# The opening of the causal attention layer: key-side bias tiles made by TensorE transposes of the query-side ones, one 2 MB trip through DRAM on SyncE's queue, rows of x ahead of the bias

## The chip, the cores and the metric

One core of a Trainium2 chip runs the whole program. The metric is the device time of one execution in microseconds (us); the median of three executions before the change is 2824.74 us.

## What is computed

Eight layers in a row on x of 4 x 1024 x 128: a scan layer, an expert layer, a landmark attention layer, an expert layer, **a causal attention layer with rotary positions and a relative bias**, an expert layer, a memory attention layer, an expert layer. The change lies in the fifth alone:

```python
q, k, v = heads(x @ Wq + bq), heads(x @ Wk + bk), heads(x @ Wv + bv)   # x normalised first; 16 heads of 8
q, k = q * cos + rotate_half(q) * sin, k * cos + rotate_half(k) * sin
bias = rel_bias_table[bucket(pos_i - pos_j)]                           # 32 buckets, 16 heads
att = (q @ k.T + bias) / sqrt(8), causal mask, softmax
x = x + (att @ v) @ Wp + bp
```

## The kernel before

The layers follow one another, each between barriers of all engines, so what one layer saves at its start the program saves. X stays in SBUF as `g.X`, with mean and variance of its rows in `g.MV`.

The causal layer (`causal_layer`, from L1040) works in 16 units `u`: 4 sequences times 4 groups of 4 heads. TensorE (PE), VectorE (DVE), ScalarE (ACT) and SyncE (SP, which issues the DMAs) each run the same `walk` of steps in the same order, each with its own body for a step. Two PSUM slots of two banks, `slot(n)`, are used in turn by all steps that carry a number n; PE claims a slot when the step two before has freed it.

- `turn_x`: DVE makes the normalised rows `xn` of one sequence (L1510; POOL does it for the later three, L1291), PE turns them (L1393), ACT copies them into `xt` (L1316).
- `project`: PE multiplies by Wq or Wk and its swapped copy (L1400), DVE adds bias and rotation (L1520) and sums (L1525) into `full`.
- `split`: ACT and DVE cut `full` into three bf16 pieces (L1326, L1532, L1329, L1536), and SP stores each piece in DRAM (L1239).
- `stack`: SP waits until the six pieces of the sequence are stored, then loads the operands of one unit as 72 rows for the query side (three DMAs, L1252) and 72 for the key side (three, L1255) into `stacks`.
- `values`: PE makes v (L1407), ACT copies it (L1333).
- `top`: 32 steps a unit; PE makes scores of 128 queries (L1419), DVE takes their maxima, far part by L1566 and near part with the bias `bias_q` by L1567. `join` and `lower` bring the maxima into the stacks as three further rows (L1585, L1425, L1262).
- `scores`, `products`, `copy_y` and so on: scores with bias, exp, times v.

The opening is the walk up to `lower(0)`: x of sequence 0, q and k, the stacks of units 0 to 2, v, and the 32 tops of unit 0, which nothing overlaps. Units 1 to 15 have their tops between the scores of the unit before.

The bias needs tiles whose row p is the bias vector of a head shifted by p. PE picks the vectors from the table by a one-hot product for two sides (L1380), DVE copies them (L1497, L1498), SP stores them in DRAM (L1267). ACT then copies DRAM to DRAM with one row of 1 KB for each shift, in four DMAs of 1 MB: half of the heads at a time, side 1 and side 0 (L1305). SP loads them in two halves (`load_bias`, L1232): `bias_q` for the maxima and two key-side parts, the even heads for `bias_k` (kept in `pt`) and the odd heads for `bias_kd`. Half 0 is loaded ahead of the walk; half 1 after the stack loads of unit 0. ACT and DVE cut `bias_k` into three bf16 pieces `bias_kp` for PE to add (L1310, L1541, L1312, L1544), half 0 in `values`, half 1 on DVE in the middle of the tops of unit 0 (`t == ROWS // 2`).

## Time and profile before

| | |
|---|---|
| median of 3 executions | 2824.74 us (2817.64 to 2830.39) |
| the profiled execution | 2821.07 us, its span 2819.1 us |
| busy share of the span | PE 80%, DVE 65%, PE weight load 58%, ACT 51%, POOL 31% |
| mean granted clock of TensorE | 0.865 of full speed |
| causal layer, first instruction to last statistics | 819.2 to about 1686 us |
| its opening, up to PE's step of `lower(0)` | 819.2 to 921.7 us |
| the other stretch, up to 1690 us | 768.3 us |

Times of the trace are microseconds from the start of the span. A gap of an engine stands in brackets with what ended it. DMA share is the busy share of the core's 16 DMA engines.

### The profile page before, as it was taken

What the parts mean: (1) busy time and instruction counts of PE and PEld (TensorE: products, weight loads), DVE (VectorE), ACT (ScalarE), POOL (GpSimd) and SP (SyncE); (2) the same over time, 40 slices, a digit from 0 to 9 for tenths busy, and PEclk for the clock granted to TensorE, in tenths of its full rate; (3) what the DMA queues carried; (4) which work ended last, traced back from release to release, by engine and by line L of the source; (5) the groups of instructions that cost most, each with busy time, mean ns of one, the idle gap of its engine ahead of it and who ended that gap; (6) DMA issues with size and microseconds to landing.
All of it is one profiled execution on the core that took longest, in us unless ns stands there. A gap on an engine that the chain in (4) does not pass through costs nothing. (4 is left out here: it accounts for less than half of the span.)

```text
span 2819.1 us, 79607 instructions
## 1 busy us (share of the span) xinstructions
PE 2250.5 (80%) x30676; PEld 1640.9 (58%) x30676; DVE 1820.5 (65%) x5861; ACT 1425.0 (51%) x3583; POOL 865.8 (31%) x852
## 2 busy tenths in 40 slices
PE   6489947589934888798888877948888888888786
PEld 3389924479921333333333337936777777777686
DVE  5533356633335777777777633359999999999533
ACT  4366632366621445445454544635555555555264
POOL 2157620057741100000000002624444444443255
PEclk8589977689965898989989886969999999999688
DMA  3011120011135211111110001121111111111113
GB/s 123 30 38 49 47 68 0 30 35 49 48 126 153 74 32 35 29 30 35 33 43 18 18 3 47 46 84 50 51 50 49 48 50 45 48 48 47 41 39 90
DMA packets 81721, 139.72 MB, mean 50 GB/s; under 512 B 18691, under 2 KB 37803, under 8 KB 78924
## 3 DMA queue, kind: packets, MB, share of 16 engines
q1 hardware_dynamic: 62244, 101.88, 11.6%
q0 software_dynamic: 13824, 28.34, 3.5%
q8 instruction: 250, 4.10, 0.6%
q10 hardware_dynamic: 5288, 4.46, 0.5%
q14 instruction: 115, 0.94, 0.1%
HBM read 69.69 MB, written 35.18 MB: 37 GB/s over the span
## 5 line engine op out<-in xcount | busy, mean ns | idle before, releaser
L1353 ACT ACTIVATE ca_pt<-ca_ps 128x512 f32<-128x512 f32 (+3 forms) x768 | 341.1, 491 | 369.6 <-PE ca_ps L1445 168.2
L668 PE MATMUL ffn_ps<-ffn_xst,ffn_up_w 128*128 128x128 f32 x3456 | 430.0, 279 | 0.2 <-issue 0.2
L668 PEld LDWEIGHTS ffn_ps<-ffn_xst,ffn_up_w 128*128 128x128 f32 x3456 | 411.8, 196 | 1.2 <-issue 1.2
L782 DVE TENSOR_TENSOR ffn_hid<-ffn_sg,ffn_ps 128x512 f32<-128x512 f32 x216 | 148.5, 688 | 363.1 <-PE ffn_ps L668 360.2
L540 POOL DMA_INDIRECT ffn_xs<-ffn_x,ffn_token_at x216 | 209.1, 968 | 256.7 <-DVE ffn_token_at L765 192.1
L1419 PE MATMUL ca_ps<-ca_stacks 72*128 72x512 bf16 (+3 forms) x768 | 230.1, 367 | 64.9 <-DVE ca_m_near L1567 31.3
L1774 POOL TENSOR_TENSOR im_pt_e<-im_pt,im_own 128x512 f32<-128x512 f32 x128 | 162.6, 1270 | 384.9 <-DVE im_pt L2027 367.0
L1441 PE MATMUL ca_ps<-ca_stacks 75*128 75x512 bf16 (+3 forms) x768 | 254.0, 354 | 19.2 <-ACT ca_pt L1353 11.2
L1566 DVE TENSOR_REDUCE ca_m_far<-ca_ps 128x1 f32<-128x128 f32 (+5 forms) x384 | 236.6, 616 | 47.1 <-PE ca_ps L1419 45.5
L545 POOL DMA_INDIRECT ffn_y<-ffn_ys,ffn_result_at x216 | 212.6, 984 | 153.7 <-DVE ffn_ys L788 146.1
L1567 DVE CUSTOM_DVE_ANT_0 ca_spill<-ca_ps,ca_bias_q 128x256 f32<-128x256 f32 (+1 forms) x512 | 200.7, 397 | 35.8 <-PE ca_ps L1419 35.8
L1463 PE MATMUL ca_ps<-ca_pt,ca_vp 128*9 128x512 f32 (+3 forms) x1536 | 181.9, 548 | 43.2 <-ACT ca_ysb L1361 43.2
L509 POOL MEMSET ffn_later<- 128x128 f32 x4 | 0.8, 206 | 697.0 <-POOLq L42 697.0
L1781 POOL TENSOR_TENSOR im_rope_qk<-im_t,im_mates 128x512 f32<-128x512 f32 x128 | 170.6, 1333 | 56.8 <-DMA im_mates<-im_t 56.0
L1419 PEld LDWEIGHTS ca_ps<-ca_stacks 72*128 72x128 bf16 x768 | 67.9, 103 | 199.6 <-DVE ca_m_near L1567 100.2
L1580 DVE TENSOR_TENSOR ca_ps<-ca_ps,ca_bias_kd 128x256 f32<-128x256 f32 (+1 forms) x288 | 109.8, 382 | 98.1 <-PE ca_ps L1441 94.6
L1807 ACT ACTIVATE im_ot<-im_ps 128x256 f32<-128x256 f32 x128 | 49.1, 383 | 241.4 <-PE im_ps L1870 241.4
L598 ACT ACTIVATE ffn_up_w<-w_w 128x1024 f32 x144 | 151.9, 1056 | 29.3 <-issue 26.8
L1441 PEld LDWEIGHTS ca_ps<-ca_stacks 75*128 75x128 bf16 x768 | 78.9, 103 | 146.2 <-ACT ca_pt L1353 71.9
L591 ACT ACTIVATE ffn_sg<-ffn_ps 128x512 f32<-128x512 f32 x216 | 128.9, 597 | 59.9 <-PE ffn_ps L668 59.8
L1821 ACT ACTIVATE im_pe_<-im_s,im_nm 128x32 f32<-128x32 f32 x512 | 157.0, 316 | 1.9 <-DVE im_nm L2036 1.9
L676 PE MATMUL ffn_ps<-w_w,ffn_hid 128*128 x1152 | 152.4, 276 | 1.2 <-DVE ffn_ys L788 1.2
(318 smaller groups left out, 4873.0 us busy)
## 6 DMA issues: line engine op xcount, KB each, us to landing
im_mates<-im_t SPq DMA_DIRECT2D x256, 128.0 KB
ca_stacks<-scratch_piece SPq DMA_DIRECT2D x96, 192.0 KB
ffn_got<-ffn_y SPq DMA_DIRECT2D x48, 256.0 KB, 5.7
ffn_x<-ffn_xn SPq DMA_DIRECT2D x32, 256.0 KB, 2.0
scratch_piece<-ca_piece SPq DMA_DIRECT2D x24, 256.0 KB, 2.9
w_w<-in_L_ffn_experts_w_dram SPq DMA_DIRECT2D x2, 2048.0 KB, 12.4
scratch_toeplitz<-scratch_bias ACTq DMA_DIRECT2D x4, 1024.0 KB
ffn_xs<-ffn_x,ffn_token_at POOLq DMA_INDIRECT x216, 2.5
```

The lines of the kernel that those rows point to most:

```text
L540: nc.gpsimd.indirect_dma_start(out=xs[:, n % XS, :], out_offset=None, in_=xn_rows[:, :], in_offset=bass.IndirectOffsetOnAxis(ap=token_at[: ...
L545: nc.gpsimd.indirect_dma_start(out=y_rows[:, :], out_offset=bass.IndirectOffsetOnAxis(ap=result_at[:, n:n + 1], axis=0), in_=ys[:, n % YS, ...
L668: last = nc.tensor.matmul(ps[:, bank, j * P:j * P + P], up_w[:, n % WS, first + j * P:first + j * P + P], xst[:, n % 2, :], start=True, st ...
L1353: nc.scalar.activation(pt[:, i % 8, lo - c0:hi - c0], ps[:, tile_bank(i), lo - c0:hi - c0], ACT.Exp, scale=SCALE).then_inc(p_ready, 1)
L1419: last = nc.tensor.matmul(slot_row(n)[:, c:e], stacks[0:KD, u % 3, 0, j, qt * P:qt * P + P], stacks[0:KD, u % 3, 1, j, c:e], start=True, s ...
L1441: last = nc.tensor.matmul(ps[:, tile_bank(i), lo - c0:hi - c0], stacks[:, u % 3, 1, j, kt * P:kt * P + P], stacks[:, u % 3, 0, j, lo:hi], ...
L1463: nc.tensor.matmul(ps[32 * j:32 * j + D + 1, 7, lo - c0:hi - c0], vp[:, b % 2, kt, gr * G4 + j, :], pt[:, i % 8, lo - c0:hi - c0], start=( ...
L1566: nc.vector.tensor_reduce(m_far[:, u % 2, t:t + 1], slot_row(n)[:, 0:lo], AX_X, ALU.max)
L1567: nc.vector.tensor_tensor_reduce(spill[:, n % 2, 0:hi - lo], slot_row(n)[:, lo:hi], bias_q[:, h, W2 - (hi - lo):W2], 1.0, NEG, ALU.add, AL ...
L1774: nc.gpsimd.tensor_tensor(pt_e[:, j % 2], pt[:].unsqueeze(2).to_broadcast(shape), own[:].unsqueeze(1).to_broadcast(shape), ALU.mult).then_ ...
L1781: nc.gpsimd.tensor_tensor(rope_qk[:, k % 2].rearrange("p a b -> p (a b)"), t1[:], mates[:, k % 2, :], ALU.subtract).then_inc(S["rope_ready ...
L1821: last = nc.scalar.activation(pe_[:, h, :], s1[:, h, :], ACT.Exp, bias=nm[:, h:h + 1], accum_out=sm[:, j % 2, h:h + 1])
```

## The change

Only the vectors of side 1 are made (one product at L1380's place, one copy of 16 x 384). SP stores them, waits, issues **one** DMA of 2048 rows of 1 KB from DRAM to DRAM, waits for it, and loads all 16 heads of `bias_q` with one DMA of 2 MB; ACT issues no DMA any more. A new step `turn_bias` stands in the walk between `values` and the first `top`, once for each group of 4 heads: PE turns 8 blocks of 128 x 128 of `bias_q` into a slot, ACT copies the even heads to `bias_kp` in bf16 and the odd ones to `bias_kd`, DVE subtracts, ACT makes the second piece, DVE the third. The two `split_bias` and the second `load_bias` are gone. On DVE the reciprocal and the eight `xn` tiles of sequence 0 come before the copy of the bias vectors; on PE the products for the zero row and for the output bias move behind the projections into `values`; the weights have a semaphore of their own.

```diff
@@ sync
-                    sp.dma_start(w[:, i, :], m).then_inc(loaded, 16)
+                    sp.dma_start(w[:, i, :], m).then_inc(w_loaded, 16)
...
-                    if u == 0:
-                        load_bias(1)
...
-                sp.wait_ge(bias_made, 2)
-                sp.dma_start(dram_bias.rearrange("a h n -> h a n"), bias_rows).then_inc(bias_stored, 16)
-                load_bias(0)
+                sp.wait_ge(bias_made, 1)
+                sp.dma_start(dram_bias, bias_rows).then_inc(bias_stored, 16)
+                sp.wait_ge(bias_stored, 16)
+                sp.dma_start(dram_toeplitz, bass.AP(dram_bias.tensor, P - 1, [[384, H], [-1, P], [1, W2]])).then_inc(toeplitz_stored, 16)
+                sp.wait_ge(toeplitz_stored, 16)
+                sp.dma_start(bias_q[:], dram_toeplitz.rearrange("h p w -> p h w")).then_inc(bias_loaded, 16)
                 sp.wait_ge(filled, 6)
                 walk(split=split, stack=stack, lower=lower)
@@ scalar
-                act.wait_ge(bias_stored, 16)
-                for half in range(2):
-                    lo = half * H // 2
-                    for side, offset in ((1, P - 1), (0, P)):
-                        rows = bass.AP(dram_bias.tensor, (side * H + lo) * 384 + offset, [[384, H // 2], [-1, P], [1, W2]])
-                        act.dma_start(dram_toeplitz[side, lo:lo + H // 2], rows).then_inc(toeplitz_stored[half], 16)
...
+                def turn_bias(gr, n):
+                    heads = slice(gr * G4 // 2, gr * G4 // 2 + G4 // 2)
+                    turned = slot_row(n).rearrange("p (h r w) -> p r h w", r=2, w=W2)
+                    act.wait_ge(slot_filled, n + 1)
+                    nc.scalar.activation(bias_kp[:, 0, heads], turned[:, 0], ACT.Copy).then_inc(bias_copied, 1)
+                    nc.scalar.activation(bias_kd[:, heads], turned[:, 1], ACT.Copy).then_inc(bias_copied, 1)
+                    act.wait_ge(bias_rest1, gr + 1)
+                    nc.scalar.activation(bias_kp[:, 1, heads], bias_rest[:, gr], ACT.Copy).then_inc(bias2, 1)
@@ tensor
                 def project(b, side, h, n):
                     pe.wait_ge(xt_ready, b + 1)
+                    pe.wait_ge(w_loaded, 16 * 6)
...
+                def turn_bias(gr, n):
+                    pe.wait_ge(bias_loaded, 16)
+                    claim(n)
+                    for j in range(G4):
+                        for r in range(2):
+                            c = j * W2 + (1 - r) * P
+                            last = nc.tensor.transpose(slot_row(n)[:, c:c + P], bias_q[:, gr * G4 + j, r * P:r * P + P], g.ident[:])
+                    last.then_inc(slot_filled, 1)
@@ vector
                 def turn_x(b, n):
                     if b == 0:
                         for t in range(TB):
...
                         last.then_inc(xn_ready, 1)
-                        dve.wait_ge(bias_row_made, 1)
-                        nc.vector.tensor_copy(bias_row[:], ps[:, S0, 0:P]).then_inc(bias_row_ready, 1)
+                        dve.wait_ge(slot_filled, 1)
+                        nc.vector.tensor_copy(bias_rows, ps[0:H, 0, 0:384]).then_inc(bias_made, 1)
+                        dve.wait_ge(bias_made, 1)
+                        dve.sem_inc(slot_free[0], 1)
+                        dve.wait_ge(loaded, 16 * 7)
+                        nc.vector.tensor_copy(bv_wide[:], bv_col[:].to_broadcast([P, P])).then_inc(bv_spread, 1)
...
+                def turn_bias(gr, n):
+                    heads = slice(gr * G4 // 2, gr * G4 // 2 + G4 // 2)
+                    turned = slot_row(n).rearrange("p (h r w) -> p r h w", r=2, w=W2)
+                    dve.wait_ge(bias_copied, 2 * gr + 2)
+                    nc.vector.tensor_tensor(bias_rest[:, gr], turned[:, 0], bias_kp[:, 0, heads], ALU.subtract).then_inc(bias_rest1, 1)
+                    dve.wait_ge(bias_rest1, gr + 1)
+                    dve.sem_inc(slot_free[n % 2], 1)
+                    dve.wait_ge(bias2, gr + 1)
+                    nc.vector.tensor_tensor(bias_kp[:, 2, heads], bias_rest[:, gr], bias_kp[:, 1, heads], ALU.subtract).then_inc(bias_split, 1)
...
-                    if t == ROWS // 2 and u == 0:
-                        split_bias(1)
```

On ACT, from the table load of the layer's first instruction on, before:

```order
L1299 ACTIVATE ca_std<-g_mv,g_eps 128x32
L1305 DMA scratch_toeplitz<-scratch_bias 1024x1x256 x4
L1316 ACTIVATE ca_xt<-ca_ps 128x1024
L1326 ACTIVATE ca_piece<-ca_full 128x1024
L1329 ACTIVATE ca_piece<-ca_full 128x1024
```

and after the change:

```order
L1294 ACTIVATE ca_std<-g_mv,g_eps 128x32
L1307 ACTIVATE ca_xt<-ca_ps 128x1024
L1317 ACTIVATE ca_piece<-ca_full 128x1024
L1320 ACTIVATE ca_piece<-ca_full 128x1024
L1317 ACTIVATE ca_piece<-ca_full 128x1024
L1320 ACTIVATE ca_piece<-ca_full 128x1024
L1324 ACTIVATE ca_vp<-ca_ps 128x128x8
L1300 ACTIVATE ca_bias_kp<-ca_ps 128x512
L1301 ACTIVATE ca_bias_kd<-ca_ps 128x512
L1303 ACTIVATE ca_bias_kp<-ca_pt 128x512
```

The four issues that stood ahead of the copy of xt are gone; three copies of 128 x 512, four times over, stand behind the copy of v.

On SP, from the store of the bias vectors on, before:

```order
L1267 DMA scratch_bias<-ca_pt 16x2x384
L1232 DMA ca_bias_q<-scratch_toeplitz 128x8x256
L1232 DMA ca_pt<-scratch_toeplitz 128x4x256
L1232 DMA ca_bias_kd<-scratch_toeplitz 128x4x256
L1239 DMA scratch_piece<-ca_piece 16x8x1024 x6
L1252 DMA ca_stacks<-scratch_piece 24x1x4096 x3
L1255 DMA ca_stacks<-scratch_piece 24x4096 x3
L1232 DMA ca_bias_q<-scratch_toeplitz 128x8x256
L1232 DMA ca_pt<-scratch_toeplitz 128x4x256
L1232 DMA ca_bias_kd<-scratch_toeplitz 128x4x256
L1252 DMA ca_stacks<-scratch_piece 24x1x4096 x3
```

and after the change:

```order
L1259 DMA scratch_bias<-ca_pt 16x384
L1261 DMA scratch_toeplitz<-scratch_bias 2048x1x256
L1263 DMA ca_bias_q<-scratch_toeplitz 128x16x256
L1233 DMA scratch_piece<-ca_piece 16x8x1024 x6
L1246 DMA ca_stacks<-scratch_piece 24x1x4096 x3
L1249 DMA ca_stacks<-scratch_piece 24x4096 x3
L1246 DMA ca_stacks<-scratch_piece 24x1x4096 x3
```

The copy from DRAM to DRAM now stands in SP's row ahead of the stores of the pieces, and the stack loads of the three units follow one another with no bias load between.

On PE, from the product that picks the bias vectors to the first top, before:

```order
L1380 MATMUL ca_ps<-ca_pt,ca_table 16x384 x2
L1382 MATMUL ca_ps<-ca_pt,g_ones 128x512
L1386 MATMUL ca_ps<-ca_w,ca_bv_wide 128x128
L1387 MATMUL ca_ps<-ca_brow,g_ones 128x128
L1393 MATMUL ca_ps<-g_ident,ca_xn 128x128 x8
L1400 MATMUL ca_ps<-ca_xt,ca_w 128x512 x8
L1407 MATMUL ca_ps<-ca_w,ca_xt 128x128 x8
L1419 MATMUL ca_ps<-ca_stacks 128x128
```

and after the change:

```order
L1367 MATMUL ca_ps<-ca_pt,ca_table 16x384
L1373 MATMUL ca_ps<-g_ident,ca_xn 128x128 x8
L1381 MATMUL ca_ps<-ca_xt,ca_w 128x512 x8
L1386 MATMUL ca_ps<-ca_pt,g_ones 128x512
L1390 MATMUL ca_ps<-ca_w,ca_bv_wide 128x128
L1391 MATMUL ca_ps<-ca_brow,g_ones 128x128
L1395 MATMUL ca_ps<-ca_w,ca_xt 128x128 x8
L1406 MATMUL ca_ps<-g_ident,ca_bias_q 128x128 x32
L1417 MATMUL ca_ps<-ca_stacks 128x128
```

The turns of x stand right behind the one product that is left, and 32 turns of the bias stand between v and the first top.

## Rows read from the trace of the kernel before

**Rows 1.** Windows: us, busy us per engine (count), PEclk, DMA share, GB/s.
```profile
819.20:921.70 102.50, 41.09 (x98) 14.07 (x98) 49.02 (x123) 13.28 (x13) 22.92 (x17) 0.55 0.53 148
921.70:1690.00 768.30, 654.68 (x4248) 271.87 (x4248) 537.39 (x1844) 378.53 (x824) 19.68 (x34) 0.89 0.12 32
```

**Rows 2.** Timeline of PE: start us, us, instruction, idle before it.
```profile
822.54 2.74 PE L1380 MATMUL ca_ps<-ca_pt,ca_table 33*16 33x384 f32 x4 [33.69 <-DMA ca_pt<-in_buckets_dram]
...
832.77 1.97 PE L1393 MATMUL ca_ps<-g_ident,ca_xn 128*128 128x128 f32 x8 [0.40 <-DVE ca_xn L1510]
845.56 7.10 PE L1400 MATMUL ca_ps<-ca_xt,ca_w 128*128 128x512 f32 x12 [10.82 <-ACT ca_xt L1316]
...
890.71 0.50 PE L1419 MATMUL ca_ps<-ca_stacks 72*128 72x128 bf16 x2 [25.87 <-DMA ca_stacks<-scratch_piece]
...
921.71 0.39 PE L1425 MATMUL ca_ps<-g_ident,ca_m_all 128*32 128x128 f32 x1 [1.69 <-DVE ca_m_all L1585]
```

**Rows 3.** Timeline of ACT at the start of the layer.
```profile
820.58 0.32 ACT L1299 ACTIVATE ca_std<-g_mv,g_eps 128x32 f32<-128x32 f32 x1
830.16 14.28 ACTq L1305 DMA_DIRECT2D scratch_toeplitz<-scratch_bias  x4
844.48 1.02 ACT L1316 ACTIVATE ca_xt<-ca_ps 128x1024 f32<-128x1024 f32 x1 [23.58 <-issue]
```

**Rows 4.** Timeline of DVE, from the norms to the last piece of k.
```profile
826.47 0.35 DVE L1502 RECIPROCAL ca_rstd<-ca_std 128x32 f32<-128x32 f32 x1
830.06 0.67 DVE L1505 COPY ca_bv_wide<-ca_bv_col 128x128 f32<-128x128 f32 x1 [3.24 <-DMA ca_bv_col<-in_L_attn_a_bv_dram]
830.20 2.51 DVE L1510 TENSOR_SCALAR ca_xn<-g_x,g_mv,ca_rstd 128x128 f32<-128x128 f32 x8
...
849.14 1.41 DVE L1520 SCALAR_TENSOR_TENSOR ca_rot<-ca_ps,ca_bcol,ca_cs 128x512 f32<-128x512 f32 x2 [16.24 <-PE ca_ps L1400]
850.59 0.69 DVE L1525 TENSOR_TENSOR ca_full<-ca_rot 128x512 f32<-128x512 f32 x1
...
852.76 2.17 DVE L1525 TENSOR_TENSOR ca_full<-ca_rot 128x512 f32<-128x512 f32 x1
...
867.44 1.22 DVE L1536 TENSOR_TENSOR ca_piece<-ca_full,ca_piece 128x1024 bf16<-128x1024 f32 x1 [1.12 <-ACT ca_piece L1329]
```

**Rows 5.** Timeline of POOL: what runs beside DVE's long sum.
```profile
852.03 2.35 POOL L1295 TENSOR_TENSOR g_x<-g_x,ca_bias_row 128x1024 f32<-128x1024 f32 x1
```

**Rows 6.** Timeline of SP's DMA issues.
```profile
826.35 0.34 SPq L1267 DMA_DIRECT2D scratch_bias<-ca_pt  x1
844.29 0.38 SPq L1232 DMA_DIRECT2D ca_bias_q<-scratch_toeplitz  x1
...
871.65 2.35 SPq L1252 DMA_DIRECT2D ca_stacks<-scratch_piece  x3
```

**Rows 7.** Windows of 2 us: the copy in DRAM alone, then beside bias loads.
```profile
838.00:840.00 2.00, 0.00 (x0) 0.00 (x0) 0.00 (x0) 0.00 (x0) 0.00 (x0) 0.50 0.54 191
...
850.00:852.00 2.00, 2.00 (x5) 0.68 (x4) 1.93 (x4) 0.00 (x0) 1.95 (x3) 1.00 1.09 381
```

**Rows 8.** A later stack load: its first issue, and DMA at its end.
```profile
1025.13 2.28 SPq L1252 DMA_DIRECT2D ca_stacks<-scratch_piece  x3
...
1038.00:1039.00 1.00, 0.97 (x4) 0.29 (x4) 1.00 (x5) 0.49 (x2) 0.00 (x0) 1.00 0.18 74
```

**Rows 9.** Timeline of DVE in the middle of the tops of unit 0.
```profile
904.49 1.22 DVE L1541 TENSOR_TENSOR ca_pt<-ca_pt,ca_bias_kp 128x1024 f32<-128x1024 f32 x1
906.84 1.23 DVE L1544 TENSOR_TENSOR ca_bias_kp<-ca_pt,ca_bias_kp 128x1024 bf16<-128x1024 f32 x1 [1.12 <-ACT ca_bias_kp L1312]
907.98 0.28 DVE L1567 CUSTOM_DVE_ANT_0 ca_spill<-ca_ps,ca_bias_q 128x128 f32<-128x128 f32 x1
```

**Rows 10.** Windows of two units with the same steps, at two clocks.
```profile
1265.00:1304.10 39.10, 34.23 (x260) 14.40 (x263) 31.41 (x115) 22.31 (x50) 0.00 (x0) 1.00 0.13 32
...
1453.50:1497.60 44.10, 39.58 (x260) 15.60 (x263) 31.67 (x114) 22.41 (x50) 0.00 (x0) 0.85 0.11 28
```

More of the change, by code:

```diff
@@ L1057, in idle, with walk @@
         pass
-    def walk(turn_x=idle, project=idle, split=idle, values=idle, stack=idle, top=idle, join=idle, lower=idle,
+    def walk(turn_x=idle, project=idle, split=idle, values=idle, turn_bias=idle, stack=idle, top=idle, join=idle, lower=idle,
              scores=idle, products=idle, copy_y=idle, gather_y=idle, turn_y=idle, out=idle):
@@ L1073, in walk @@
         n += 1
+        for gr in range(NG):
+            turn_bias(gr, n)
+            n += 1
         def maxima(v, first, count):
@@ L1223, in _ @@
                 sp.dma_start(bv_col[:], bv.rearrange("(p a) -> p a", a=1)).then_inc(loaded, 16)
-                def load_bias(half):
-                    sp.wait_ge(toeplitz_stored[half], 32)
-                    lo = half * H // 2
-                    tiles = dram_toeplitz[0, lo:lo + H // 2].rearrange("(h r) p w -> r p h w", r=2)
-                    lo2 = lo // 2
-                    for bias, src in ((bias_q[:, lo:lo + H // 2, :], dram_toeplitz[1, lo:lo + H // 2].rearrange("h p w -> p h w")),
-                                      (bias_k[:, lo2:lo2 + H // 4, :], tiles[0]), (bias_kd[:, lo2:lo2 + H // 4, :], tiles[1])):
-                        sp.dma_start(bias, src).then_inc(bias_loaded[half], 16)
                 def split(b, side, part):
@@ L1367, in turn_y @@
                     act.sem_inc(slot_free[n % 2], 1)
-                walk(turn_x=turn_x, split=split, values=values, scores=scores, copy_y=copy_y, turn_y=turn_y)
+                walk(turn_x=turn_x, split=split, values=values, turn_bias=turn_bias, scores=scores, copy_y=copy_y, turn_y=turn_y)
             @block.tensor
@@ L1487, in out @@
                     last.then_inc(slot_filled, 1)
-                walk(turn_x=turn_x, project=project, values=values, top=top, lower=lower, scores=scores, products=products,
+                walk(turn_x=turn_x, project=project, values=values, turn_bias=turn_bias, top=top, lower=lower, scores=scores, products=products,
                      gather_y=gather_y, turn_y=turn_y, out=out)
@@ L1624, in out @@
                     ch.link(nc.vector.tensor_copy(g.MV[:, b * TB:b * TB + TB, :], mv8[:]))
-                walk(turn_x=turn_x, project=project, split=split, top=top, values=values, join=join, lower=lower, scores=scores, gather_y=gather_y, out=out)
+                walk(turn_x=turn_x, project=project, split=split, top=top, values=values, turn_bias=turn_bias, join=join, lower=lower, scores=scores, gather_y=gather_y, out=out)
         s.clear()
@@ L2187, in bucket @@
         return min(16 + int(big), 31)
[L2189 removed]
+    pick = np.zeros((33, 384), np.float32)
     for u in range(384):
[L2191 to L2196 removed]
+        n = 255 - u
+        if n < 0:
+            pick[32, u] = -1.0e30
+        else:
+            pick[bucket(n), u] += 1.0
+            pick[31, u] -= 1.0
     freq = 10000.0 ** (-np.arange(0, 64, 2, dtype=np.float64) / 64)
```

79 lines of the change are left out of this document (24 added, 55 removed).

## The prediction

> **What bounds the kernel now.** The windows come first, to see what the layer's opening is worth: 102.5 us of the layer pass before `lower(0)`, at a DVE that is busy for 49 us and a PE busy for 41, so no engine is full and the opening is a chain of waits; the 768.3 us behind it run at a granted clock of 0.89 and are none of the change's business [rows 1]. Next the timelines of the four engines, read backwards from the first top. PE starts the tops at 890.71 after 25.87 us in which a DMA, the stack loads, was the last to come [rows 2]. SP issued these loads at 871.65, when the last stored piece had landed [rows 6]. The last piece was made by DVE at 867.44 + 1.22 = 868.66, the end of a chain that DVE began at 849.14 with the rotation of q [rows 4]. That waited for PE's projections from 845.56 on [rows 2], these for ACT's copy of xt at 844.48, and in front of this copy stands no work but 14.28 us of issuing four DMAs, from 830.16 on; the gap of 23.58 us is marked "issue" [rows 3]. The turned x had been ready since 832.77 + 1.97 = 834.74 [rows 2]. And these issues waited for the stored bias vectors (issued at 826.35, rows 6), which have nothing to do with x. So the bias, by way of ACT's queue, sets the time at which q and k are made; this is what the reader should see.
>
> **The change part by part.**
>
> *x first.* The std is ready at 820.58 + 0.32 = 820.90 [rows 3]; the reciprocal costs 0.35 and the eight tiles 2.51 [rows 4], so xn is ready at 823.8. PE's product of the bias vectors is released by a DMA at 822.54 and took 2.74 for two sides [rows 2]; one side, 1.37, ends at 823.9. Turns 1.97 [rows 2], to 825.9. The copy of xt takes 1.02 [rows 3] and is now held by nothing: 827.0. From PE's start of the projections to DVE's first rotation before passed 849.14 - 845.56 = 3.58: 830.7. DVE has another condition, the small loads: the copy of bv_col was released at 830.06 and takes 0.67 [rows 4], 830.7 as well. Both give 830.7 in place of 849.14, **18.4 us earlier**.
>
> *From there to the stack loads.* The chain from the first rotation to the last piece took 19.52 us. I keep it. Of PE's twelve matmul records there the first four took the 3.58 us, the other eight 7.10 - 3.58 = 3.5, or 1.8 for four [rows 2], since the clock rose; if it rises a pair later now, that is +1.8. And it had a sum of 2.17 us instead of 0.69 [rows 4] while POOL ran its own 2.35 us addition [rows 5]; POOL now waits for `bias_row`, made behind k, so this 1.5 us goes. The two cancel within 0.3. Last piece at 850.2, first stack issue (868.66 to 871.65 before: 3.0) at **853.2**.
>
> *The two trips of the bias, now on SP.* SP's load list before the store is the same, so the vectors are stored at about 830.1 as before and the DRAM copy is issued at 830.15. Before, its first 2 MB let SP go on at 844.29 [rows 6], 14.1 us. While it ran alone the DMA engines were 0.54 busy at 191 GB/s; with SP's bias loads beside it, 1.09 and 381 [rows 7]. So each of those copies kept to half of the 16 engines. Its outermost count was 8 heads; the q side of a stack, whose outermost count is 3, ends on a share of 0.18, three engines of 16 [rows 8]. With 16 heads outermost I take all 16: 2 MB at 381 GB/s is 5.5 us, with about 2 us ahead and behind 7.6; the load of `bias_q` costs the same. `bias_q` is there at 830.15 + 7.6 + 8 = 846. If the copy keeps to half of the engines, 844.3 + 8 = 852. SP stands in the waits meanwhile with the q pieces queued behind it, the first ready at about 837.6; they go out between 838 and 845, before k's last piece at 850.2 either way. So this costs nothing, or, if the bias load lies in front of all six stores until 852, the 1.5 MB of pieces behind it at 381 GB/s: 852 + 4.1 + 1 is 857, 4 us later than 853.2.
>
> The Trainium skill ("DMA: Bandwidth & Descriptors", "Why a DMA increments its semaphore by 16 and not by 1") says that a transfer goes to the largest number of engines up to 16 that divides the slowest dimension of both sides. By it the copy goes from 8 engines to 16, and the trace's 0.54 and 0.18 agree.
>
> *turn_bias.* It is new work between v and the first top. For one group of heads: ACT two copies and later a third, each half of a 1.02 us copy [rows 3], say 0.6; DVE two operations of 0.69 [rows 4]; they wait for each other in turn, 3 x 0.6 + 0.7 + hand-overs of 0.1 = 2.7 us a group, since the last subtraction lies beside the next group's copies. PE's eight turns, 1.97 [rows 2], lie beside it. ACT comes to it after the copy of v, about 850.3, or when `bias_q` is there and turned, 848 to 854. Four groups end at 851 + 4 x 2.7 + 0.8 = 863, at the latest 867. The stacks of unit 0 are not there before 867 (below), so all of it is hidden; were they there, each us past them would count in full.
>
> *The stack loads.* From the first issue to the first top passed 890.71 - 871.65 = 19.1 us, with a 2 MB bias load issued behind them. Now the loads of units 1 and 2 stand behind them instead. A later stack that loads alone was issued at 1025.13 and ended at 1039 [rows 8], 14 us. The opening's row is nearer, for there is again a queue behind: 19.1, bounds 14 and 24 (5 more). Tops start at 853.2 + 19.1 = **872.3 instead of 890.7: 18.4 us**.
>
> *The tops.* DVE's second bias split in their middle goes: 907.98 - 904.49 = **3.5 us** [rows 9]. PE and DVE do the rest as before. Stacks of units 1 and 2 end at about 881 and 890 and are wanted from 900 on.
>
> ACT's issues, the store of the second side and 2 MB of DRAM copy vanish too; beyond the above they lay beside other work. The 768.3 us behind `lower(0)` are left at zero, bounded below.
>
> **Sum**: 18.4 + 3.5 = 21.9 us. Against the profiled execution, 2821.07 - 21.9 = 2799.2; this execution was 3.7 us under the median of 2824.74, and the forecast goes by the median: 2824.7 - 22 = **2802.7 us**, 0.8% less. A measurement of this kernel can tell about 0.5%, 14.1 us, from no change.
>
> **The rivals.**
>
> *The bias load behind them is what stretched the stacks.* Then they land in 14 us, tops start at 867.2, behind the turns of the bias if only just: gain 23.5 + 3.5 = 27, 2798. For it: the lone stack. Against: two further stacks now queue, whose rows go to the same partitions.
>
> *SP's queue becomes the chain.* Both 2 MB trips go at the 191 GB/s of the old copy: the first ends at 844.3, the second takes 13 and ends at 857.4, the six stores drain in its wake until 862.5, tops start at 881.6. Gain 9.1 + 3.5 = 12.6, 2812. For it: the stores now share a queue with 2 MB loads, which the copy in ACT's queue never did to them. Against: 381 GB/s from the same two kinds of transfer [rows 7].
> The Trainium skill ("DMA: Bandwidth & Descriptors", "Issuing engines are not separate DMA queues") holds that a second issuing engine only saves sequencer time, usually small; by it alone removing ACT's issues would give almost nothing and the gain would be the 3.5 us of the tops. The 14.28 us in rows 3 speaks against "small" here, and I give that reading no more than what the trace gives it: part of the last case below.
>
> *The clock takes it back.* Two units with the same steps took 39.1 us at a clock of 1.00 and 44.1 at 0.85 [rows 10]. The 15 units after the opening stand at 0.89 on average; were all of them at 0.85, 0.04 x (44.1 - 39.1) / 0.15 x 15 is 20 us, and the change would show nothing, about 2823. For it: the opening shifts when PE's work comes. Against: these units repeat one another from batch to batch, so their clock comes from their own load.
>
> *Slower.* The new DRAM copy is spread over few engines, as the q side of the stacks is over three. At half of the engines 2 MB took about 11 us, so three need 30: stored at 861, `bias_q` at 869, six stores drained at 874.5, tops at 893.6; with the 3.5 us this is 0.6 us better than before, so three engines is the point from which it decides. With two, 45 us: 15 us slower, 2839. For it: nothing but that the transfer's shape is new. Against: its sibling with 8 heads outermost ran on half of the engines.
>
> **How the numbers follow.** Forecast 0.55, shorter stacks 0.15, SP's queue 0.15, clock or another unseen loss that leaves less than 14 us 0.10, slower by the fewer engines or the like 0.05. Range: from 2798 less 4 us of spread between executions, 2794, to the 2812 of SP's queue and 1 more, 2813; the clock case and the slower one lie outside. Faster by over 0.5%: 0.55 + 0.15 + about a third of SP's queue, less some for the spread, is 0.78; within 0.5%: 0.17; slower: 0.05.
>
> **What would show it.** ACT's copy of xt at 826 to 828; DVE's first rotation at 830 to 831; first stack issue at 852 to 855, or at 857 to 863 if SP's queue holds it; DMA share near 1 from 832 to 837 (0.5 until 843 would mean half of the engines); the turns of the bias over by 867; the first top 18 to 20 us after the first stack issue, with DMA stacks as the last wait; no split inside the tops, and `lower(0)` 27.5 us after the first top; units 0 to 15 as long as before. It is wrong if the first top waits for DVE's or ACT's part of `turn_bias`, or if the stretch behind `lower(0)` is off 768 us by more than 5.

## The result: twice the forecast gain, two thirds of it in a layer that the change does not touch

The changed kernel takes **2781.98 us** (median of 4 runs, 2772.17 to 2788.15), the kernel before beside it 2823.26 (2817.64 to 2830.39): a ratio of 0.986 with an interval of 0.983 to 0.990. The gain is 41 us where 22 were forecast, and the time lies 12 us below the range.

The two profiled executions have spans of 2819.1 and 2770.4 us; that of the changed kernel is the fastest of its four, 10 us under their median. From the first and last record of each layer, the 48.7 us between them are (0.4 us lie in the gaps):

| stretch | before | after | gain |
|---|---|---|---|
| start to the causal layer | 819.3 | 815.3 | 4.0 |
| **opening, up to `lower(0)`** [rows 1] | 102.4 | 91.1 | **11.3** |
| rest of the causal layer | 763.8 | 767.1 | -3.3 |
| expert layer | 170.6 | 170.9 | -0.3 |
| **memory layer** | 786.5 | 753.4 | **33.1** |
| last expert layer | 152.6 | 149.1 | 3.5 |

The windows of the changed kernel (opening, rest of the layer, memory layer; columns as in [rows 1]), then the memory layer of the kernel before:

```profile
815.30:906.40 91.10, 43.62 (x128) 17.65 (x128) 56.16 (x126) 15.57 (x21) 23.86 (x17) 0.59 0.41 119
906.40:1673.50 767.10, 659.26 (x4248) 272.85 (x4248) 535.59 (x1838) 377.39 (x822) 17.12 (x18) 0.89 0.12 32
1847.40:2600.80 753.40, 655.75 (x19872) 551.07 (x19872) 702.85 (x2171) 428.11 (x1549) 338.57 (x269) 0.97 0.15 51
```

```profile
1859.20:2645.70 786.50, 671.61 (x19872) 563.20 (x19872) 720.22 (x2172) 428.04 (x1549) 334.77 (x269) 0.95 0.14 49
```

The memory layer has the same instructions in both. So there are two stories: why the opening gave 11.3 of 21.9 us, and why a layer that nobody touched gave 33. The -3.3 us of the rest of the causal layer tell nothing: over the 18 traces of this case that stretch takes 762.7 to 779.0 us, the four longest at a mean granted clock of 0.870 to 0.874, the four shortest at 0.891 to 0.894, and the unchanged kernel before alone has 763.8 and, profiled again, 779.0.

**The opening.** Timelines of the changed kernel: PE, ACT, DVE, POOL, SP, the rows that answer to [rows 2 to 4] and [rows 6].

```profile
827.62 1.97 PE L1373 MATMUL ca_ps<-g_ident,ca_xn 128*128 128x128 f32 x8 [8.13 <-DVE ca_xn L1501]
830.71 7.21 PE L1381 MATMUL ca_ps<-ca_xt,ca_w 128*128 128x512 f32 x12 [1.11 <-ACT ca_xt L1307]
...
878.70 0.50 PE L1417 MATMUL ca_ps<-ca_stacks 72*128 72x128 bf16 x2 [18.49 <-DMA ca_stacks<-scratch_piece]
...
906.45 0.40 PE L1423 MATMUL ca_ps<-g_ident,ca_m_all 128*32 128x128 f32 x1 [1.69 <-DVE ca_m_all L1581]
```

```profile
829.63 1.02 ACT L1307 ACTIVATE ca_xt<-ca_ps 128x1024 f32<-128x1024 f32 x1 [12.66 <-PE ca_ps L1373]
...
850.28 1.06 ACT L1317 ACTIVATE ca_piece<-ca_full 128x1024 bf16<-128x1024 f32 x1 [8.06 <-DMA scratch_piece<-ca_piece]
```

```profile
817.39 10.18 DVE L1501 TENSOR_SCALAR ca_xn<-g_x,g_mv,ca_rstd 128x128 f32<-128x128 f32 x8
...
834.40 1.41 DVE L1517 SCALAR_TENSOR_TENSOR ca_rot<-ca_ps,ca_bcol,ca_cs 128x512 f32<-128x512 f32 x2 [6.01 <-PE ca_ps L1381]
...
847.00 0.69 DVE L1522 TENSOR_TENSOR ca_full<-ca_rot 128x512 f32<-128x512 f32 x1
...
864.36 0.74 DVE L1548 TENSOR_TENSOR ca_bias_kp<-ca_pt,ca_bias_kp 128x512 bf16<-128x512 f32 x1 [0.69 <-ACT ca_bias_kp L1303]
```

```profile
816.08 10.70 POOL L1274 MEMSET ca_stacks<- 11x4096 bf16 x3
```

```profile
829.56 0.65 SPq L1261 DMA_DIRECT2D scratch_toeplitz<-scratch_bias  x1
839.55 0.38 SPq L1263 DMA_DIRECT2D ca_bias_q<-scratch_toeplitz  x1
840.05 15.50 SPq L1233 DMA_DIRECT2D scratch_piece<-ca_piece  x6
858.60 2.33 SPq L1246 DMA_DIRECT2D ca_stacks<-scratch_piece  x3
```

ACT's 23.58 us of "issue" [rows 3] are gone: its copy of xt now waits for PE. But PE waited 8.13 us for xn, whose eight tiles took 10.18 us instead of 2.51 [rows 4]: they stand in the same 10 us as POOL's memsets of the stacks. Before, xn came at 830.20, when these memsets were ending (timeline of POOL, before):

```profile
820.02 10.63 POOL L1279 MEMSET ca_stacks<- 11x4096 bf16 x3
```

And ACT's first cut of k (850.28) waited for a DMA, the stores of q, though its input was complete at 847.00 + 0.69: they were issued from 840.05 on, behind the 2 MB load of `bias_q`.

**The memory layer.** It runs 128 equal steps. In each, DVE makes two products `im_t`, SP copies the first with the rows swapped into `mates` (128 KB, two DMAs), POOL combines copy and second product into `im_rope_qk`, and DVE later makes `im_uu`. Groups of instructions in that layer (busy us, mean ns, idle before), first before, then after:

```profile
L1781 POOL TENSOR_TENSOR im_rope_qk<-im_t,im_mates 128x512 f32<-128x512 f32 x128 | 170.6, 1333 | 56.8 <-DMA im_mates<-im_t 56.0
L2045 DVE TENSOR_TENSOR im_uu<-im_lift,im_u 128x256 f32<-128x256 f32 x128 | 96.9, 757 | 3.3 <-issue 0.4
L1855 PEld LDWEIGHTS im_ps<-im_rope_qk 64*32 64x32 f32 x4096 | 36.1, 106 | 110.3 <-issue 59.4 <-POOL im_rope_qk L1781 50.3
```

```profile
L1777 POOL TENSOR_TENSOR im_rope_qk<-im_t,im_mates 128x512 f32<-128x512 f32 x128 | 174.4, 1362 | 60.9 <-DMA im_mates<-im_t 60.0
L2041 DVE TENSOR_TENSOR im_uu<-im_lift,im_u 128x256 f32<-128x256 f32 x128 | 78.9, 617 | 3.0
L1851 PEld LDWEIGHTS im_ps<-im_rope_qk 64*32 64x32 f32 x4096 | 36.0, 105 | 93.7 <-issue 78.8 <-POOL im_rope_qk L1777 14.5
```

One operation of DVE got 18 us cheaper without being changed. It takes 0.42 to 0.72 us, unless it starts while POOL's `im_rope_qk` runs: then, in 35 of 36 cases before and 9 of 10 after, it ends 0.28 us behind that operation, and takes up to 1.52. All 284 `im_uu` of over 1 us in the 18 traces are of this kind. Where `im_uu` starts first, POOL's operation takes the longer, up to 1.54 us instead of 1.28. Timelines of POOL and DVE around the same `im_uu` in both (number 66, counted from 0), before:

```profile
2265.49 1.28 POOL L1774 TENSOR_TENSOR im_pt_e<-im_pt,im_own 128x512 f32<-128x512 f32 x1 [2.58 <-DVE im_pt L2027]
2266.73 1.27 POOL L1781 TENSOR_TENSOR im_rope_qk<-im_t,im_mates 128x512 f32<-128x512 f32 x1
```

```profile
2266.93 1.35 DVE L2045 TENSOR_TENSOR im_uu<-im_lift,im_u 128x256 f32<-128x256 f32 x1
```

and after:

```profile
2242.31 1.27 POOL L1770 TENSOR_TENSOR im_pt_e<-im_pt,im_own 128x512 f32<-128x512 f32 x1 [2.59 <-DVE im_pt L2023]
2244.92 1.28 POOL L1777 TENSOR_TENSOR im_rope_qk<-im_t,im_mates 128x512 f32<-128x512 f32 x1 [1.34 <-DMA im_mates<-im_t]
```

```profile
2243.74 0.43 DVE L2041 TENSOR_TENSOR im_uu<-im_lift,im_u 128x256 f32<-128x256 f32 x1
```

What reads like a loss is the gain: after the change POOL waits 1.34 us for the copy of the mates, `im_rope_qk` so starts behind `im_uu` and not on top of it, and from this `im_uu` to the next pass 5.49 us instead of 6.09. Of the 128 `im_uu`, 31 lasted over 1 us before and 9 after; 24 of the 31 in steps of the form 4k + 2. In the kernel before, a step that begins with a long one takes 6.53 us on average, another 5.63, so 22 fewer of them are 20 of the 33 us. About half of these 0.9 us goes with the clock: between steps wholly at the full granted clock the difference is 0.42 us, but 12 of the 31 long steps stand at least in part at the lower granted clock (0.5 of full speed, 1.2 GHz), 3 of the 96 others, and in all 54 us of the steps before and 17 after. The other 13 us are mostly in the steps without a long `im_uu`, which take 5.53 us after; why is not shown.

Why is the copy late there? It is that of step 68, two ahead of this `im_uu`. The view of the DMA queues (packets, MB, share of 16 engines) for the 2 us behind its second `im_t`, in which the copy runs, before (2264.2 to 2266.2) and after (2241.0 to 2243.0):

```profile
q1 hardware_dynamic: 160, 0.26, 35.8%
```

```profile
q1 hardware_dynamic: 155, 0.25, 34.7%
q8 instruction: 1, 0.02, 5.2%
q14 instruction: 1, 0.01, 1.7%
```

A packet of the queue "q8 instruction" fell into the copy. The page of the kernel before has this row, that of the changed one the same:

```profile
q8 instruction: 250, 4.10, 0.6%
```

250 packets of 16.4 KB. The trace holds 64,467 records of TensorE (matmuls, weight loads, semaphores) before: one packet per 258, from which I take it that this queue brings TensorE's program; the runs below, which lengthen the program, bear it out. The Trainium skill ("Advanced Engine Details and Errata", ISA Cache) gives a line of 16 KB, 256 instructions; the count agrees. I paired packets with landings in steps 4 to 123: with a packet in flight between 0.6 and 2.3 us behind a step's second `im_t` the mates land 2.81 us behind it on average (61 steps before), without one 2.13 (59 steps); after, 2.79 and 2.12. Of the landings later than 2.9 us, 25 of 28 and 29 of 31 had a packet. Four steps have some 1275 records of TensorE, five packets, so the late landing keeps to the same step of four: 15 of the 28 late ones in steps 4k + 1 before, 17 of 31 in steps 4k after (`im_rope_qk` is two steps ahead of the `im_uu` it meets). Ahead of the layer TensorE has 21,434 records before and 21,498 after: the 32 transposes of `turn_bias` with their weight loads, less the two matmuls of the second bias side and theirs, plus four waits, 64 more. Two explanations were tested. **Theory F**: those 64 instructions moved the fetches by a quarter of a packet. **Rival E**: the layer differs by something else that is left behind (addresses, queue contents, the time at which it begins).

### The profile page after: what moved, and what is told of

Same layout as the page of the kernel before. It is cut to its first block and busy times, and to the rows that moved or that the text cites. A ratio compares the mean times of both kernels' runs of the same rounds, so it can differ in the third digit from the quotient of the medians.

```text
span 2770.4 us, 79676 instructions
## 1 busy us (share of the span) xinstructions
PE 2233.2 (81%) x30706; PEld 1626.5 (59%) x30706; DVE 1809.5 (65%) x5864; ACT 1427.8 (52%) x3591; POOL 870.2 (31%) x852
## 5 line engine op out<-in xcount | busy, mean ns | idle before, releaser
L1439 PE MATMUL ca_ps<-ca_stacks 75*128 75x512 bf16 (+3 forms) x768 | 256.5, 358 | 18.4 <-ACT ca_pt L1341 13.1
```

The lines of the kernel that those rows point to most:

```text
L1439: last = nc.tensor.matmul(ps[:, tile_bank(i), lo - c0:hi - c0], stacks[:, u % 3, 1, j, kt * P:kt * P + P], stacks[:, u % 3, 0, j, lo:hi], ...
```

## The experiments

The runs were made in four series; in the last two the expert layers take longer, some 320 us instead of 295 for each of the first two (the kernel before: 2898 and 2900 us), and the causal and memory layers do not, so the text compares ratios and stretches of layers. rep_before, rep_after, after_pad256, after_pad64, both_moves, stack_alone and two_halves are single executions, whose totals carry no interval. Where the opening is left alone, it takes 102.4 to 103.0 us in the kernel before (4 traces) and 90.0 to 91.5 in the changed one (7 traces), so what a move gives there is told as a range. "Opening" is from the layer's first record to `lower(0)`, "steps" from the first `im_uu` to the last.

**Both kernels again.**

> The kernel before, unchanged, profiled once more. Of the 41 us that the change gave, the two profiled executions put 11.3 into the causal layer's opening and 33 into the memory layer, which the change does not touch (786.5 us before, 753.4 after). Theory A: each program has its own rhythm in the memory layer, so this one takes 786 +- 4 again and the whole 2817 to 2830. Theory B: that layer's time is drawn anew in each execution; then it may come out anywhere from 750 to 790 and the whole shifts with it.

> The changed kernel, unchanged, profiled once more. Theory A: memory layer 753 +- 6 again, whole 2772 to 2788. Theory B: anywhere from 750 to 790. The opening up to lower(0) is 91.1 us from the layer's first instruction in either case, within 1.

2836.23 and 2778.49 us. Memory layer 784.3 and 753.5, opening 103.0 and 90.0: the 31 us belong to the kernels, not to the execution. The whole of rep_before lies 6 us above what was expected: its rest of the causal layer took 779.0 us.

**memset_later.**

```diff
+                pool.wait_ge(xn_ready, 1)
                 for k in range(3):
                     pool.wait_ge(filled, 2 + k)
```

> The changed kernel with one wait on POOL: its three memsets of the stacks start only when the eight xn tiles are made. If the memsets on POOL are what stretched the xn tiles on DVE (10.18 us beside them, 2.51 without), these take 2.5 us again and x is turned 7.7 us sooner. Theory 1, the chain goes through x alone: first stack issue and first top 7 to 8 us sooner, opening 83.5. Theory 2, SP's queue takes over: the q pieces are then stored behind the 2 MB load of bias_q, ACT waits for them before it cuts k, and only 3 to 4 us of the 7.7 are left, opening 87.5. If xn still takes 10 us, both fall.

2776.55 us, ratio 0.985 (0.981 to 0.989). Its timelines of DVE, ACT and SP:

```profile
819.96 2.14 DVE L1502 TENSOR_SCALAR ca_xn<-g_x,g_mv,ca_rstd 128x128 f32<-128x128 f32 x8
```

```profile
849.47 1.06 ACT L1318 ACTIVATE ca_piece<-ca_full 128x1024 bf16<-128x1024 f32 x1 [12.38 <-DMA scratch_piece<-ca_piece]
```

```profile
838.37 0.38 SPq L1263 DMA_DIRECT2D ca_bias_q<-scratch_toeplitz  x1
838.87 15.88 SPq L1233 DMA_DIRECT2D scratch_piece<-ca_piece  x6
```

xn takes 2.14 us without the memsets, so they cost it 8. q's rotation is 7.9 to 8.1 us earlier, the opening only 1.9 to 3.1 shorter (88.0, beside 90.0 in rep_after and 91.1 in the changed kernel): ACT now waits 12.38 us for q's stores, which still leave SP behind the load of `bias_q`. The Trainium skill ("Trainium Architecture — The Big Picture", What this means for kernel authors) says that inside SBUF's engine side only DVE and GpSimd contend, by an exclusive lock. The trace of the changed kernel agrees: behind each of the three memsets two tiles end, 0.09 and 0.15 us later, however early they began. Not every operation is held: the reciprocal takes 0.35 us inside a memset and without one, and the copies of the bias vectors from PSUM, 0.55 us, end in the middle of a memset in the kernel before.

**bias_behind_q.** The load of `bias_q` moves behind q's three stores.

```diff
-                sp.dma_start(bias_q[:], ...).then_inc(bias_loaded, 16)
...
+                    if (b, side, part) == (0, 0, 3):
+                        sp.wait_ge(toeplitz_stored, 16)
+                        sp.dma_start(bias_q[:], ...).then_inc(bias_loaded, 16)
```

> The changed kernel with one issue moved: SP loads bias_q behind the three stores of the q pieces instead of ahead of them. Theory: in the changed kernel ACT's first cut of k waited 2.5 us for the q pieces (850.28 against k's sum at 847.69), since their stores stood in the same queue behind the 2 MB load. With the load behind them this wait goes, first stack issue and first top 2 to 3 us sooner, opening 88.5; the turns of the bias start at about 853 and end at about 867, still ahead of the stacks. Rival: the wait is for the stores' own 2.9 us of landing and nothing changes, opening 91.

2780.66 us, ratio 0.985 (0.981 to 0.989). k's first cut starts 32.4 us into the layer instead of 34.5 to 34.9, the opening is 88.6: 1.3 to 2.5 us shorter, the small term that was expected. The totals of this run and of memset_later can't be told from the changed kernel's 0.986; these readings rest on the openings.

**both_moves, stack_alone, all_moves.** Both moves at once; then SP issuing each of the first stacks only when the one before has landed; then all three.

```diff
                 def stack(u):
                     b, gr = u // NG, u % NG
+                    if u in (1, 2):
+                        sp.wait_ge(stacks_loaded[u - 1], 2 * NP * 16)
```

> The changed kernel with GpSimd's memset of the stacks behind the normalisation of x, and the 2 MB load of bias_q behind q's stores. Alone, the one took 1.9 us off the stretch up to the first lower (89.95 to 88.0), because q's stores still stood behind the load, and the other 1.3. If the two hide each other's gain (theory: two waits in a row, of which the second ends last), together they take 7 to 9 us: first lower at 81 to 83 us. If not, the sum of the two: 86.7.

> The changed kernel in which SyncE issues the stack of unit 1 only when that of unit 0 has landed (and unit 2's when unit 1's has). Theory: the first stack takes 20 us from issue to the first top because the loads of units 1 and 2 share the 16 engines with it; alone it takes some 14, the first top is 5 to 6 us earlier and the first lower at 84 to 86 us. Rival: the transfer of 12 packets rows is bound by its own small packets (its own engines' rate), not by what is queued behind: first top at 62 us as before.

> The changed kernel with all three: memsets behind the normalisation, the load of bias_q behind q's stores, and each of the first stacks alone. TensorE's program keeps its length, so the memory layer should stay at 750 to 760 us (theory F). Opening 76 to 80 us if the three add up, the total 10 to 14 us under the changed kernel, 2766 to 2772 us. Rival: the load of bias_q, moved behind q's stores, now ends beside the first stack and holds it up, or turn_bias ends last: opening 82 to 86, total 2775.

Openings 82.2, 85.7 and **76.4** us. The two moves give 1.9 to 3.1 and 1.3 to 2.5 us alone and 7.8 to 9.2 together: two waits in a row, of which only the later one is seen. The stack alone is there 15.4 us after its issue instead of 19.7 to 20.8. Timeline of SP, stack_alone, where the second stack waits for the first:

```profile
914.21 2.33 SPq L1248 DMA_DIRECT2D ca_stacks<-scratch_piece  x3
916.59 1.39 SPq L1251 DMA_DIRECT2D ca_stacks<-scratch_piece  x3
929.57 2.18 SPq L1248 DMA_DIRECT2D ca_stacks<-scratch_piece  x3
```

all_moves has the lowest ratio here: 2840.76 us beside 2897.74 of the kernel before on the same chip, 0.981 (0.978 to 0.985). That interval touches those of the changed kernel (0.983 to 0.990, and 0.982 to 0.993 later); its opening is shorter by 15 us.

**after_pad192, before_pad64, after_pad256, after_pad64.** Increments of a semaphore that nothing waits for, at the head of TensorE's program in the memory layer.

```diff
+                for _ in range(192):
+                    pe.sem_inc(S["pad"], 1)
                 for c in range(2 * BATCH):
```

> The changed kernel with 192 increments of an unused semaphore at the head of TensorE's program in the memory layer, where TensorE waits some 5 us anyway. Theory F (place of the instruction fetches): the 16,384 B packets on the queue that loads TensorE's instructions come once per about 256 of its instructions (250 packets, 64,467 records in the trace of before). They delay the copy of the mates in the step in which they fall, and so decide whether GpSimd's im_rope_qk meets VectorE's im_uu. The change made TensorE's program ahead of this layer 64 instructions longer (21,498 records against 21,434); 192 more complete a packet of 256 and put the fetches back where the kernel before has them. F expects the memory layer at 780 to 790 us instead of 753.5, im_uu at 740 to 770 ns instead of 617, and a total near 2810 us. Rival E (what the causal layer leaves behind, such as addresses, tables of constants, queue contents or the time at which the layer begins): the layer stays at 750 to 757 us and the total at 2780.

> The kernel before with 64 such increments at the head of TensorE's program in the memory layer. Theory F: the fetches fall where the changed kernel has them, so the memory layer takes 750 to 760 us instead of 785, and the total is near 2790 us, 30 less than before with nothing in the causal layer touched. Rival E: layer 780 to 790 us, total 2815 to 2825.

> Control: the changed kernel with 256 increments, a whole packet more, so that the fetches fall where they fell. Theory F: memory layer 750 to 760 us (plus up to 5 us at its head if the increments outlast TensorE's wait there). A third theory, D, by which any delay at the head or any longer program of TensorE upsets the steps, expects it as slow as with 192.

> The changed kernel with 64 increments: fetches another quarter of a packet later, a place that neither kernel has had. Theory F gives no sign for it, only that it may differ from both 753 and 785 us, and that the step (by number modulo 4) with the late mates moves again; rival E expects 750 to 757.

2846.91 (ratio 1.007, 1.005 to 1.009), 2812.59 (0.996, 0.994 to 0.998), 2824.10 and 2813.09 us. The totals mislead, and those that were expected are missed: TensorE was thought to wait there, but an increment takes 0.153 us, so the layer's head grew from 30.8 us to 60.3, 40.7, 69.9 and 40.5. The steps behind it tell: 739.3, 726.9, 714.6 and 734.5 us. Theory F has its two large signs (192 slow, 256 fast), which E and "any delay" do not give. before_pad64 went half of the way: its layer took 780.2 us, 9.8 of them the longer head, where F expected 750 to 760 and E 780 to 790. In after_pad64 the late copies moved on to steps 4k + 3 (15 of 33), as F had it.

**before_ca64, after_again, after_hidden192.** The same with the increments hidden: before_ca64 has 64 in the wait ahead of the first top; after_hidden192 has 96 there and 96 at the end of TensorE's program in the next expert layer.

```diff
                 def top(u, t, n):
+                    if t == 0 and u == 0:
+                        for _ in range(64):
+                            pe.sem_inc(pad, 1)
```

> The kernel before with 64 increments of an unused semaphore on TensorE, now placed in its 25.9 us wait ahead of the causal layer's first top, where 64 of them (0.155 us each at the head of the memory layer, 9.9 us in all) cost nothing. From there on TensorE's instruction fetches fall as in the changed kernel; nothing else of the change is made. Theory F: the memory layer's 127 steps take 710 to 727 us instead of 743, the causal layer stays at 866, total 2795 to 2812 us (before: 2826). Rival E (something else that the change leaves behind): steps 740 to 745, total 2820 to 2830.

> The changed kernel unchanged, so that the next three have it timed on their own chip: ratio to before 0.986, the memory layer's 127 steps at 710 us.

> The mirror image of the 64 increments in the kernel before: the changed kernel with 192 unused increments on TensorE where it waits anyway, 96 ahead of the causal layer's first top (14.9 us inside a wait of 18.5) and 96 behind TensorE's last instruction of the expert layer that follows (14.9 us inside a wait of 20.6). Theory F: fetches fall as in the kernel before, the memory layer's steps take 735 to 743 us instead of 710, the head stays at 31, and the total is 25 to 32 us over the changed kernel: ratio to before 0.996 to 0.998. Rival E (the change gave more than the fetches' place): steps at 710 to 720, ratio 0.986 to 0.989.

before_ca64: 2873.72 us beside 2897.74, ratio **0.990 (0.986 to 0.994)**: 64 increments that nothing needs, and the kernel is 24 us faster, 15 to 17 of them in the memory layer. (The profiled execution is the slowest of the four: its causal layer took 878 us, not the 866 that were expected.) after_hidden192: 2879.07 beside 2859.23 of after_again (ratios to before 0.993 and 0.988), 20 us slower, 5 less than the least expected. Two groups of the memory layer (busy, mean, idle before), in before_ca64, after_again and after_hidden192:

```profile
L2048 DVE TENSOR_TENSOR im_uu<-im_lift,im_u 128x256 f32<-128x256 f32 x128 | 85.3, 667 | 3.3 <-issue 0.4
L1858 PEld LDWEIGHTS im_ps<-im_rope_qk 64*32 64x32 f32 x4096 | 36.2, 106 | 100.4 <-issue 72.2 <-POOL im_rope_qk L1784 27.9
```

```profile
L2041 DVE TENSOR_TENSOR im_uu<-im_lift,im_u 128x256 f32<-128x256 f32 x128 | 77.5, 606 | 2.9
L1851 PEld LDWEIGHTS im_ps<-im_rope_qk 64*32 64x32 f32 x4096 | 36.5, 106 | 92.0 <-issue 78.6 <-POOL im_rope_qk L1777 13.0
```

```profile
L2048 DVE TENSOR_TENSOR im_uu<-im_lift,im_u 128x256 f32<-128x256 f32 x128 | 94.2, 736 | 2.9
L1858 PEld LDWEIGHTS im_ps<-im_rope_qk 64*32 64x32 f32 x4096 | 36.1, 106 | 108.1 <-issue 61.4 <-POOL im_rope_qk L1784 45.9
```

before_ca64 lies between the kernels (757 and 617 ns, 50.3 and 14.5 us behind POOL). after_hidden192 has the picture of the kernel before back, row by row: 736 ns, 45.9 us behind POOL, 28 long `im_uu`.

**all_moves_ca32 and two_halves.** The three moves with 32 increments ahead of the first top; and the changed kernel with its DRAM copy as two copies of 8 heads.

```diff
-                sp.dma_start(dram_toeplitz, bass.AP(dram_bias.tensor, P - 1, [[384, H], ...])).then_inc(toeplitz_stored, 16)
-                sp.wait_ge(toeplitz_stored, 16)
+                for lo in (0, H // 2):
+                    sp.dma_start(dram_toeplitz[lo:lo + H // 2], bass.AP(..., [[384, H // 2], ...])).then_inc(toeplitz_stored, 16)
+                sp.wait_ge(toeplitz_stored, 32)
```

> The three moves (memsets later, load of bias_q behind q's stores, each of the first stacks alone) and 32 increments ahead of the first top, an eighth of a packet. Theory F says only that the memory layer moves: between 711 us (none) and 734 us (64 of them), unless a still better place lies there. The total is 12 to 15 us under the changed kernel if the steps stay at 711, and 0 to 5 if they go to 725.

> The changed kernel with its DRAM to DRAM copy as two copies of 8 heads each. A copy with 16 as its first size ran on 16 engines in 10 us; if the first size sets the number of engines (as the forecast had it), each of the two runs on 8, both start together and share them, and the copy takes about 14 us as the eight-head copies of the kernel before did: the load of bias_q is issued at 27 to 28 us of the layer instead of 23.8, and the first lower moves by at most 1 us, since turn_bias waits for nothing else and ends 12 us ahead of the first top. Rival: 2 copies overlap and spread over 16 engines, issue at 24.

2848.04 us, ratio 0.983 (0.978 to 0.988), opening 75.3, steps 720.7, between those of the same kernel without increments (711.1) and of the changed one with 64 (734.5). two_halves: 2869.54 us. Its timeline of SP:

```profile
889.27 2.23 SPq L1262 DMA_DIRECT2D scratch_toeplitz<-scratch_bias  x2
903.23 0.38 SPq L1264 DMA_DIRECT2D ca_bias_q<-scratch_toeplitz  x1
```

14.0 us from issue to issue, as the copies of 8 heads took before, against 10.0 in one piece. The windows of 2 us in the middle of the copy, changed kernel and two_halves (the last two columns are DMA share and GB/s):

```profile
833.00:835.00 2.00, 2.00 (x4) 0.72 (x3) 0.60 (x1) 0.00 (x0) 0.00 (x0) 0.72 1.02 306
```

```profile
893.00:895.00 2.00, 2.00 (x4) 0.82 (x3) 0.75 (x2) 0.00 (x0) 0.00 (x0) 0.50 0.54 181
```

With 16 heads outermost all 16 engines work, with two copies of 8 half of them, though both are in flight. The opening grew by 4.8 us (96.2 beside 91.4), not by 1 at most: q's stores stand behind the copy too, ACT waits for them, and k's last piece ended 5 us later.

All kernels by the place of the fetches (TensorE's instructions ahead of the memory layer, over the kernel before, modulo 256):

| place | kernel | steps, us | `im_uu` over 1 us | copies of steps 4k with a packet, of 30 |
|---|---|---|---|---|
| 0 | before, rep_before | 743.2, 742.1 | 31, 29 | 13, 11 |
| 0 | after_pad192, after_hidden192 | 739.3, 737.3 | 23, 28 | 9, 10 |
| 64 | before_pad64, before_ca64 | 726.9, 725.2 | 17, 18 | 19, 23 |
| 64 | after, rep_after, after_again, after_pad256 | 710.3, 710.7, 709.5, 714.6 | 9, 8, 8, 14 | 26, 26, 26, 22 |
| 64 | the six variants of the opening | 710.5 to 719.6 | 9 to 13 | 22 to 26 |
| 96 | all_moves_ca32 | 720.7 | 13 | 18 |
| 128 | after_pad64 | 734.5 | 20 | 13 |

The last column ties the place to the steps. The copies of steps 4k are those that POOL waits for while DVE is at the `im_uu` of step 4k - 2, the kind that is long most often. Over the 18 traces, none of the 208 `im_uu` of that kind was long when the copy landed later than 2.9 us, and 216 of the other 314 were. So the increments moved packets into and out of these copies, and the long `im_uu` followed.

The place moves the steps by 17 us in the kernel before and by 28 in the changed one. **What stays open**: at the same place the two kernels still differ, by 16 us at 64 and by 3 to 6 at 0 (with 64 more instructions, packets fall into 19 and 23 of the 30 copies in the kernel before, into 22 to 26 in the changed one): theory F has at least half of the 33 us shown, not all. Another engine's program is fetched too (the row q14 above), and its length changed by a few instructions; that was not tried.

## Why the prediction was wrong

**The step that failed first: "The 768.3 us behind `lower(0)` are left at zero", and with them all that follows the layer.** Inside the layer this held to 3.3 us, finer than the 16 us by which that stretch varies. Behind it lay 33 us in the memory layer. 17 to 28 of them come from the length of TensorE's program (17 us by itself in the kernel before, 28 when taken back in the changed one), in which the forecast counted the transposes as work beside other work and nothing else. No rival had it, and the range, drawn around the opening, could not hold it. That the kernel came out faster by more than 0.5% is luck too: the opening's 11.3 us alone are 0.4%.

**x first, 18.4 us: 10.8.** Measured from the layer's start, the first rotation is at 19.1 us, forecast at 11.4, before at 29.9. The eight tiles were priced at 2.51 us from a row in which POOL's last memset of the stacks was ending; moved 10 us forward they run beside all three and take 10.18. Without them (memset_later) the rotation is at 11.1. A price holds for the neighbours that its row had.

**From there to the stack loads, 19.52 us kept: 20.6**, and 3.6 instead of 3.0 to the first issue. The text had q's stores queued behind the bias load and found that it "costs nothing", since they go out before k's last piece. It overlooked that ACT waits for them before it cuts k into the same tile, 2.6 us. The rival "SP's queue becomes the chain" names the right queue with the wrong price: its gain of 12.6 us is near the opening's 11.3 by chance, for the DRAM copy took 10.0 us and not the 14.1 that it assumes. memset_later shows that it was the next wait in line.

**The stack loads, 19.1 us: 20.1**, right; the rival of a shorter stack was wrong for this kernel and right about the reason, as stack_alone shows (15.4 us). **The tops, 3.5: 3.3**, right (31.0 before [rows 2], 27.75 after). **turn_bias**: 2.36 us a group for 2.7 forecast, done at 865.1, 13.6 us ahead of the first top: hidden. **The DRAM copy**: 10.0 us for 7.6 forecast, on all 16 engines as forecast. In all 10.8 - 1.1 - 0.6 - 1.0 + 3.3 is 11.4, and the opening gave 11.3 of 21.9 us.

The Trainium skill ("DMA: Bandwidth & Descriptors", Issuing engines are not separate DMA queues) calls the time to issue usually small. Here removing 14.28 us of it from ACT's queue, with x's turn moved forward, took 10.8 us off the way to the first rotation, and the 7.6 us that are missing were held by the memsets. The four issues took 1.24, 1.21, 6.23 and 5.51 us in the kernel before: the first two were short, the last two, with the earlier ones still in flight, were not.

**The clock takes it back**: the mean granted clock of the 767 us behind the opening is 0.89 as before; no.

The chances have a slip: 0.55 + 0.15 + a third of 0.15, less something for the spread, is under 0.75, not 0.78.

So the sign was right, the opening's gain half of the forecast, and the total wrong by a term from outside the layer.

## What to carry to other kernels

When operations move forward, price them beside their new neighbours: look at what the other engines, POOL's memsets above all, do at the time to which they go. When the measured gain differs from the forecast, compare every stage of the program first; if an untouched stage moved, ask what it shares with the changed one, the length of an engine's program among it, and test that with idle instructions in a hidden place. A gain of this kind is real but belongs to no edit: the next change of the program's length may take it back, so the opening's 11 us are what can be counted on as the change's own.

## What the runs showed of the hardware that was not expected

- The fetch of TensorE's instructions (one 16.4 KB packet per 258 records) goes with a later landing of a 128 KB copy inside SBUF that it falls into, 2.8 us on average instead of 2.1, and moving the fetches moves the late copies. In a loop of some 320 instructions a step it keeps returning to the same step of four, and its place decides 17 to 28 us of 743.
- A DVE operation of 0.43 us that starts inside POOL's 1.3 us operation takes up to 1.5, for it ends 0.28 us behind it; eight tiles of 2.1 us in all take 10.2 beside three memsets of 10.7, two ending 0.09 and 0.15 us behind each.
- A later landing made the program faster: 1.34 us of waiting on POOL took the collision away.
- An increment of a semaphore on TensorE takes 0.153 us: 64 add 9.7 to 9.8 us where TensorE has no wait to hide them.
